# Three-layer CIN tower on one core: turns placed later in TensorE's order, and the halves of a layer's sum added on GpSimd

## The reference

```python
h = e
for i, (W, bias) in enumerate(params):              # three layers of 200 maps
    x = einsum('bhd,bmd->bhmd', h, e).reshape(B, -1, D)
    y = relu(einsum('oi,bid->bod', W, x) + bias)
    h, direct = split(y, 2, axis=1)                 # the last layer keeps all 200 as direct
    outs.append(direct)
z = concatenate(outs, axis=1).sum(-1)               # 400 per sample
h = relu(concatenate([z, dense_ctx], 1) @ W_top1 + b_top1)
h = relu(h @ W_top2 + b_top2)
y = h @ W_top3
```

## Time and profile before

| | us |
|---|---|
| median of 3 runs | 3135.87 |
| the runs | 3124.83 to 3136.49 |
| span of the profiled execution | 3134.4 |
| TensorE matmul busy | 2930.7 (94%) |
| VectorE busy | 2622.0 (84%) |
| ScalarE busy | 1454.5 (46%) |
| GpSimd busy | 717.0 (23%) |

### The profile page before, as it was taken

How to read it: one execution, slowest core, us unless ns; L and a number is a source line. 1 busy time by engine, 2 the same in 40 slices (tenths; PEclk the granted TensorE clock), 3 DMA queues, 4 the chain that set the end, 5 groups by cost and what they waited for, 6 DMA issues and landing times.

```text
span 3134.4 us, 53996 instructions
## 1 busy us (share of the span) xinstructions
PE 2930.7 (94%) x19516; PEld 2888.7 (92%) x19516; DVE 2622.0 (84%) x1751; ACT 1454.5 (46%) x1880; POOL 717.0 (23%) x669
## 2 busy tenths in 40 slices
PE   2899999999999999999999999999999999999999
PEld 2899999999999999999999999999999999999996
DVE  4888888888888888898888888888888888988894
ACT  2554444445445444444444444444444444444452
POOL 1122222222222122222222222222221222221110
PEclk8999999999999999999999999999999999999999
DMA  6332232232332332322322322322323323323221
GB/s 149 98 89 73 79 86 71 80 83 68 90 82 68 89 78 72 90 75 73 86 77 76 90 72 76 85 73 79 87 68 83 82 68 90 79 72 89 77 66 22
DMA packets 269272, 249.87 MB, mean 80 GB/s; under 512 B 16987, under 2 KB 267786, under 8 KB 269149
## 3 DMA queue, kind: packets, MB, share of 16 engines
q1 hardware_dynamic: 200376, 196.52, 19.8%
q0 software_dynamic: 59744, 45.90, 10.2%
q10 hardware_dynamic: 9129, 7.13, 0.9%
HBM read 140.44 MB, written 4.20 MB: 46 GB/s over the span
## 4 chain that ended last, share of the span: by engine, by line
issue 58%; PE 19%; POOL 12%; DMA 8%; ACT 2%; SPq 1%; ACTq 0%; POOLq 0%; DVE 0%; DVEq 0%
PE acc L697 12%; POOL gathered L400 6%; PE acc L699 6%; POOL wait_taker L408 5%; DMA acc_copy<-acc_copy 4%; DMA gathered<-in_table,rows_now 3%; ACT acc_copy L480 1%; POOL acc_copy L409 1%; ACT y_relu L485 1%; PE z_ps L714 1%; PE hid_ps L710 1%; DMA x_pairs<-x_rows 0%; PE acc L756 0%; SPq L316 0%; PE hid_ps L779 0%
## 5 line engine op out<-in xcount | busy, mean ns | idle before, releaser
L697 PE MATMUL acc<-weights,heads 126*128 126x400 f32 (+1 forms) x9088 | 2785.6, 373 | 52.7 <-DVE tails L645 52.5
L699 PE MATMUL acc<-weights,tails 126*128 126x200 f32 (+1 forms) x9088 | 2357.8, 259 | 0.0
L697 PEld LDWEIGHTS acc<-weights,heads 126*128 126x128 f32 (+1 forms) x9088 | 1760.8, 194 | 55.5 <-issue 42.0
L699 PEld LDWEIGHTS acc<-weights,tails 126*128 126x128 f32 (+1 forms) x9088 | 1788.2, 197 | 0.0
L645 DVE TENSOR_TENSOR tails<-product,heads 126x1024 fp32r<-126x1024 f32 (+2 forms) x1152 | 1342.4, 1207 | 258.4 <-ACT heads L474 258.3
L474 ACT ACTIVATE heads<-product 126x1024 fp32r<-126x1024 f32 (+2 forms) x1152 | 1168.0, 1042 | 479.3 <-PE acc L699 339.1
L640 DVE TENSOR_TENSOR product<-hid_rep,x_rep 126x2048 f32<-126x2048 f32 x512 | 1172.8, 2291 | 103.8 <-PE acc L699 68.4
L408 POOL TENSOR_TENSOR wait_taker<-wait_taker 1x1 f32<-1x1 f32 x192 | 187.8, 978 | 2262.6 <-ACT acc_copy L480 2218.0
L485 ACT ACTIVATE y_relu<-acc_copy 128x400 f32<-128x400 f32 x192 | 103.3, 538 | 650.0 <-DMA acc_copy<-acc_copy 650.0
L480 ACT ACTIVATE acc_copy<-acc 128x800 f32<-128x800 f32 x192 | 161.3, 840 | 506.9 <-PE acc L699 501.2
L400 POOL DMA_INDIRECT gathered<-in_table,rows_now x150 | 258.1, 1721 | 45.7 <-issue 45.7
(11 more groups left out here) (27 smaller groups left out, 104.2 us busy)
## 6 DMA issues: line engine op xcount, KB each, us to landing
x_rep<-x_rows SPq DMA_DIRECT2D x512, 125.0 KB
hid_rep<-hid SPq DMA_DIRECT2D x512, 125.0 KB
x_pairs<-x_rows SPq DMA_DIRECT2D x192, 280.0 KB
acc_copy<-acc_copy POOLq DMA_DIRECT2D x192, 200.0 KB
x_pairs<-x_rows SPq DMA_DIRECT2D x64, 120.0 KB
raw_weights<-in_w ACTq DMA_DIRECT2D x12, 492.2 KB
gathered<-in_table,rows_now POOLq DMA_INDIRECT x150
x_rows<-gathered POOLq DMA_DIRECT2D x30, 80.0 KB, 3.4
```

The lines of the kernel that those rows point to most:

```text
L697: nc.tensor.matmul(acc[:, at.parity, c, 0:2 * LAYER], heads[0:rows, ring % HEADS_RING, k, cols], w, start=(q == 0 and k == 0), stop=False)
L699: last = nc.tensor.matmul(acc[:, at.parity, c, LAYER:2 * LAYER], tails[0:rows, ring % PRODUCT_RING, k, cols], w[:, 0:LAYER], start=False, ...
```

## The change

`add` no longer issues a DMA. One GpSimd instruction adds the two halves of `acc_copy` in place, 128 partitions x 400 elements, and signals `y_summed` by 1. The 1 x 1 add and its semaphore `waits_taken` go. The gathers keep their places.

On TensorE each turn moves one group back: `before` after group 1 of `first`, `l0` after group 4 (two groups back), `first` after group 3 of `second`. On ScalarE the three result operations move to match: `copy_acc` one or two `make_heads` later, `relu` behind heads that stood behind it, `copy_turned` last. VectorE and SyncE run the same lists as before.

```diff
             def add(s):
 
                 pool.wait_ge(acc_copied, s + 1)
-
-                above_zero(pool, waits_taken, s)
-                pool.tensor_tensor(wait_taker[:, 1:2], wait_taker[:, 0:1], wait_taker[:, 0:1], ALU.add).then_inc(waits_taken, 1)
-                pool.dma_start(acc_copy[:, :, 0:LAYER], acc_copy[:, :, LAYER:2 * LAYER],
-                               accum_op=ALU.add).then_inc(y_summed, 16)
+                pool.tensor_tensor(acc_copy[:, :, 0:LAYER], acc_copy[:, :, 0:LAYER], acc_copy[:, :, LAYER:2 * LAYER],
+                                   ALU.add).then_inc(y_summed, 1)
...
             def relu(layer, at, b):
-                act.wait_ge(y_summed, (at.slot + 1) * 16)
+                act.wait_ge(y_summed, at.slot + 1)
...
             def heads_and_results(slot, previous):
 
-                make_heads(*slot, 0)
-                make_heads(*slot, 1)
+                for q in range(4):
+                    make_heads(*slot, q)
                 copy_acc(*previous)
-                make_heads(*slot, 2)
-                make_heads(*slot, 3)
-                relu(*previous)
                 make_heads(*slot, 4)
                 make_heads(*slot, 5)
-                copy_turned(*previous)
+                relu(*previous)
                 make_heads(*slot, 6)
                 make_heads(*slot, 7)
+                copy_turned(*previous)
...
                 if l0 and first:
                     accumulate(*first, 0)
+                    accumulate(*first, 1)
                 if l0 and before:
                     turn(*before)
-                for q in range(1 if l0 else 0, 3) if first else ():
+                for q in (range(2, 5) if l0 else range(4)) if first else ():
                     accumulate(*first, q)
                 if before and not l0:
                     turn(*before)
                 if l0 and first:
                     turn(*l0)
-                for q in range(3, GROUPS) if first else ():
+                for q in range(5 if l0 else 4, GROUPS) if first else ():
                     accumulate(*first, q)
                 if second:
-                    for q in range(3):
+                    for q in range(4):
                         accumulate(*second, q)
                     turn(*first)
-                    for q in range(3, GROUPS):
+                    for q in range(4, GROUPS):
                         accumulate(*second, q)
```

More of the change, by code:

```diff
@@ L172, in cin_kernel @@
         taker_set = sem("taker_set")
-        waits_taken = sem("waits_taken")
         x_gathered = sem("x_gathered")
@@ L541, in split_now @@
                     return split_after(i, 1, q) if odd is None and l1 else ()
-                if before:
-                    copy_acc(*before)
                 split_heads(*split_now(0))
@@ L550, in step @@
                 if before:
-                    relu(*before)
-                if l0 and first:
-                    copy_acc(*l0)
+                    copy_acc(*before)
                 split_heads(*split_now(2))
@@ L557, in step @@
                 if before:
-                    copy_turned(*before)
+                    relu(*before)
                 if l0 and first:
-                    relu(*l0)
+                    copy_acc(*l0)
                 split_heads(*split_now(4))
@@ L563, in step @@
                     make_heads(*first, q)
+                if before:
+                    copy_turned(*before)
+                split_heads(*split_now(6))
+                if first:
+                    make_heads(*first, 6)
+                if l0 and first:
+                    relu(*l0)
+                if first:
+                    make_heads(*first, 7)
+                for q in range(2) if second else ():
+                    make_heads(*second, q)
                 if l0 and first:
                     copy_turned(*l0)
-                split_heads(*split_now(6))
-                for q in range(6, GROUPS) if first else ():
-                    make_heads(*first, q)
                 if second:
-                    heads_and_results(second, first)
+                    for q in range(2, 4):
+                        make_heads(*second, q)
+                    copy_acc(*first)
+                    make_heads(*second, 4)
+                    make_heads(*second, 5)
+                    relu(*first)
+                    make_heads(*second, 6)
+                    make_heads(*second, 7)
+                    copy_turned(*first)
             iterations(act, step)
```

## The result

The changed kernel takes 2956.88 us (2954.21 to 2958.33, 4 runs) against 3132.19 us for the kernel before, measured beside it (4 runs). The ratio is 0.9442, 95% interval 0.9426 to 0.9457: 5.6% faster. Forecast were 2936 us and a range of 2895 to 3020.

The account below looks back on a forecast made before the run. TensorE was taken as the bound, losing time in waits and at the lower clock. 61 steps x (3.78 - 0.5) = 200 us off 3134.4 gives 2934, plus 1.5 for the median: 2936 us, range 2895 to 3020.

Parts of the forecast that it names:

- The bound and the step without loss: TensorE bounds the kernel; without waits and lower clock a step takes 43.65 us instead of 47.43, a gain of 3.78.
- The chain and the turns (part 1): Copy of `acc`, add, Relu, turn: at the new places all three turns are safe by 3 us, where 2.2 were missing.
- The add (part 2): GpSimd's add of 128 x 400 takes 1.0 us, VectorE stands still meanwhile, and TensorE waits 0.5 us per step.
- T: Moment a layer ends, from which times are counted; for the turn of `before`, the end of layer 2 of the last step.
- 2a - 1.5: TensorE's new wait for tails when `before` is turned, a being the add's time: 0.5 us for a = 1, none below 0.75.
- The clock: TensorE's clock stays at 1.00 in the middle, as a wait of 0.5 us is not expected to lower it.
- a wait of 1.75 us is harmless: Read from TensorE's timeline: a wait of 1.75 us at a turn of layer 1 was not followed by the lower clock.
- The later copy of `hid` (part 3): `copy_turned(l0)` comes later, so `x_pairs` is in at T + 29.9, wanted at T + 33.6: 3.7 us left, no cost.
- Ends: Last steps: `hid` some 2.8 us later against 2.4 us back at the last Relu, counted as zero.
- 200 us forecast: Total gain: 61 full steps (60 of the loop, one unrolled) x (3.78 - 0.5) us.
- 2.8 us for `hid`: In the last steps the last layer-2 block gets its `hid` some 2.8 us later, its copy behind two more heads.
- The 2.4 us that the shorter add was to give back: The last Relu waited 3.61 us for the DMA and would wait 1.2 for an add: 2.4 back.

Follow-up runs that it names:

- e6: The GpSimd add with the turn orders of the kernel before, and a 1 x 1 add ahead of it whose end is waited for: 2909.86 us, ratio 0.9309 to before.
- e8: The changed kernel with the 1 x 1 add and a GpSimd memset of 128 x 400 in place of the add: 2916.78 us (one run), before 3118.64.
- e2: The GpSimd add in place of the DMA, with the orders of the kernel before: 2940.18 us, ratio 0.9447 to before.
- e3: The changed kernel with the GpSimd add over 200 elements instead of 400: 2927.52 us (one run), before 3114.04.
- e4: The changed kernel with a second GpSimd add of the same size ahead of the real one: 3049.66 us (one run), before 3114.04.
- e7: The changed kernel with a 1 x 1 add ahead of the GpSimd add, whose end is waited for: 2937.70 us, ratio 0.9422 to before.
- b2: The GpSimd add with the orders of the kernel before, measured again beside the changed kernel on one chip: 2942.88 us, ratio 0.9413 to before.
- a2: The changed kernel measured once more, beside other versions on one chip: 2958.43 us, ratio 0.9466 to before.

## Why the prediction was right, and where it was off

- **The bound and the step without loss.** Named rightly. The 43.65 us are 43.55 in e6 and 43.57 in e8.
- **The chain and the turns (part 1).** Right that no turn would wait. But half of the part was not needed: with the add at 1 to 2 us, the old places are early enough too (e2). I checked the new places against the new add, and never the old places against it. The change was two parts, and I did not price each alone.
- **The add (part 2).** Taken at 1.0 us; VectorE stands still for 0.86 to 0.87, and the shortest add, with nothing beside it, takes 1.03. That the exclusion works backwards was assumed, and the traces, e3 and e4 show it; e8 shows that a memset is free of it. The wait that follows was forecast as 0.5 us per step and is 44.17 - 43.55 = 0.6. But the place was wrong. I let the first add pass without cost and found the wait at the tails of group 2 of layer 1, behind the second add. It is the first add that counts. It delays the tails of group 0 of layer 1, which TensorE wants at T + 4.1, and they come at T + 2.3 + 0.9 + 1.1 = T + 4.3 and a little more. The working had both times in it (with a = 1 they come at about T + 4.4), and I did not set one against the other. The size came out near by luck: the formula 2a - 1.5 gives 0.2 for the measured a, and the wait behind the second add that it priced does not show. Only with the first wait gone does a second add cost something, 0.3 us at group 4 in e7.
- **The clock.** Right: without the long waits at the turn of layer 1 it stays at 1.00 in the loop, and the many waits of up to 1.2 us of e4 do not lower it. But that a wait of 1.75 us is harmless was read from one step. In the trace before, a wait of 1.62 us at 1653.90 is followed by a clock of 0.51 (window 1655.6 to 1659), and so are some 40 of the 58 waits of 1.5 to 3.0 us in the loop. The forecast needed only that 0.5 us are harmless, and they were.
- **The later copy of `hid` (part 3).** `x_pairs` came in time, as worked out. I followed `x_pairs` and `hid_rep`, but not `x_rep`, which stands behind both in SyncE's queue: it is late by up to 1.6 us, 54 times. It costs nothing, as e3 and e8 show.
- **Ends.** This is the term that was mis-sized. I gave the unrolled steps a gain of one full step and counted the rest as zero. Of the 200 us forecast, 59 x 3.28 = 193.5 lie in the 59 steps between the two rows, where 192.5 were measured, and 6.6 outside them. There the trace loses 14.4 us: 11.2 ahead of the loop and 3.2 in the last steps. That is 21 of the 22 us between 200 and the 178 measured. I had seen the delay in the last steps (2.8 us for `hid`), and did not ask what it does in the first ones. In the last steps it came as worked out: VectorE waits 8.93 us for the last `hid_rep`, where it waits 6.03 in e2. The 2.4 us that the shorter add was to give back do not show: with the old orders the end takes 140.2 and 139.6 us (e2, b2) against 139.8 before. What holds them was not traced.

## What to carry to other kernels

Price each part of a change alone against the chain that it shortens, and look whether that chain has the same length wherever it stands: the DMA of this one took 2.3 us at one turn and 5.6 at another. Here one part made the other superfluous, and the other then only cost time in the fill. When two engines exclude each other, ask not only how much time the add takes from the neighbour but which of its instructions stands behind it: the same 0.86 us cost 0.6 us per step ahead of both tails and nothing between them. Work the fill out by its own list of waits, since what a full pipeline covers is bare there.

## What the hardware showed that I had not expected

- The exclusion between VectorE's instructions with two inputs and GpSimd's add works in both directions, as was assumed. New is its size: VectorE loses 0.86 us to an add of 400 elements. The Trainium skill states the exclusion (SBUF — State Buffer, Who interferes with whom), and also that a GpSimd instruction which only writes is free of it; e8 shows that with 2.35 us for the tails beside a memset.
- A waiting add does not always get the next gap. In the fill of the changed kernel one was passed over five times:

```profile
142.27 8.47 POOL L405 TENSOR_TENSOR acc_copy<-acc_copy 128x400 f32<-128x400 f32 x1 [17.87 <-ACT acc_copy L476]
```

It took 8.47 us until 150.74, while VectorE ended instructions at 143.1, 144.2, 145.4, 147.6 and 148.7 and went on each time. Only at 149.8 did the add get its turn: the product that starts at 149.83 takes 2.79 us, where 2.02 is usual. In a2 one add took 8.48 us in the same step. The median of all 192 adds is 1.42 us. What decides was not tried.
